# Linear attention: one stage of 16 steps instead of two of 8, first three stacks loaded during the projection, key stacks issued on ScalarE's queue

## The reference

```
def _self_attention(x, w_qkv, w_out, heads):        # 16 heads of 16
    q, k, v = (split(z) for z in jnp.split(x @ w_qkv, 3, axis=-1))
    dots = jnp.einsum('bhie,bhje->bhij', q, k) * d ** (-0.5)
    out = jnp.einsum('bhij,bhje->bhie', dots, v)
    return out.transpose(0, 2, 1, 3).reshape(b, t, d) @ w_out

xh = x.transpose(0, 2, 1, 3).reshape(b * ww, hh, d)   # columns, weights qkv0, out0
oh = _self_attention(xh, w_qkv0, w_out0, HEADS)
xw = x.reshape(b * hh, ww, d)                         # rows, weights qkv1, out1
ow = _self_attention(xw, w_qkv1, w_out1, HEADS)
return oh + ow                                        # x = x + this, on group-normed x
```

## Time and profile before

| | |
|---|---|
| three runs | 2034.88, 2035.12 and 2040.15 us, median 2035.12 |
| span of the profiled execution | 2036.8 us; no other time of it is recorded |
| TensorE busy | 1562.8 us, 77% of the span |
| VectorE, ScalarE, GpSimd busy | 1269.2, 779.2 and 785.0 us |
| mean granted TensorE clock | 0.869 of full speed |
| queue q1 (SP) | 229.35 MB, 36.3% of the 16 transfer engines' span |
| queue q10 (ACT) | 21.31 MB, 3.3% |

### The profile page before, as it was taken

The page is one execution under the profiler, slowest core; times in us unless marked ns, Lnnn a source line. Parts: engine busy times, 40 slices in busy tenths (PEclk is TensorE's granted clock), DMA queues, the critical chain, the costliest instruction groups (busy, mean ns, idle before and its releaser), DMA issues. The chain is left out here.

```text
span 2036.8 us, 38838 instructions
## 1 busy us (share of the span) xinstructions
PE 1562.8 (77%) x13148; PEld 1212.7 (60%) x13148; DVE 1269.2 (62%) x2435; ACT 779.2 (38%) x1652; POOL 785.0 (39%) x956
## 2 busy tenths in 40 slices
PE   5958577649997587791285879947996999999990
PEld 3536464527774344461053546526886999999990
DVE  4846456566664665558224688675664777777776
ACT  2311012305453133451021336622114777777770
POOL 1531102360001440002222250014885887878770
PEclk8968788859998778895598879977997999999995
DMA  2465543354311633219331443114115656666545
GB/s 91 164 166 161 146 115 102 115 168 121 99 48 63 189 84 74 64 19 317 113 88 62 125 141 96 42 39 131 61 65 183 241 206 240 210 229 226 213 156 206
DMA packets 286766, 274.02 MB, mean 135 GB/s; under 512 B 59034, under 2 KB 263677, under 8 KB 280959
## 3 DMA queue, kind: packets, MB, share of 16 engines
q1 hardware_dynamic: 260535, 229.35, 36.3%
q10 hardware_dynamic: 17376, 21.31, 3.3%
q0 software_dynamic: 8688, 21.16, 2.8%
HBM read 194.74 MB, written 79.35 MB: 135 GB/s over the span
## 5 line engine op out<-in xcount | busy, mean ns | idle before, releaser
L787 DVE TENSOR_REDUCE a_maxima<-psum 128x2 f32<-128x512 f32 x384 | 257.5, 687 | 156.4 <-PE psum L578 88.7
L758 ACT ACTIVATE a_probs<-psum 128x512 f32<-128x512 f32 x384 | 224.6, 598 | 262.0 <-PE psum L600 167.8
L89 PE MATMUL psum<-e_x_split,e_up_split 128*128 128x256 f32 x2340 | 311.5, 282 | 7.4 <-DVE e_x_split L1749 7.4
L89 PEld LDWEIGHTS psum<-e_x_split,e_up_split 128*128 128x128 f32 x2340 | 292.5, 189 | 7.8 <-DVE e_x_split L1749 7.8
L1793 POOL TENSOR_TENSOR e_up_split<-e_up_raw,e_up_split 128x512 fp32r<-128x512 f32 x195 | 252.6, 1296 | 90.2 <-ACT e_up_split L1715 88.4
L1685 PE MATMUL psum<-e_down_split,e_hidden_split 128*128 128x256 f32 x1170 | 173.5, 284 | 0.4 <-DVE e_hidden_split L1775 0.4
L578 PE MATMUL psum<-s_k_stack,s_q_stack 96*128 96x256 bf16 x512 | 123.0, 295 | 41.6 <-DMA a_rel_stack<-scr_r 29.7
L1685 PEld LDWEIGHTS psum<-e_down_split,e_hidden_split 128*128 128x128 f32 x1170 | 152.5, 188 | 0.6 <-DVE e_hidden_split L1775 0.6
L1770 DVE TENSOR_TENSOR psum<-psum,e_silu 128x256 f32<-128x256 f32 x195 | 83.8, 430 | 106.8 <-ACT e_silu L1736 106.7
L1754 DVE TENSOR_TENSOR e_down_split<-e_down_raw,e_down_split 128x256 fp32r<-128x256 f32 x195 | 146.3, 750 | 0.0
L1039 DVE TENSOR_TENSOR a_products<-psum,mask 128x512 f32<-128x512 f32 x128 | 82.9, 686 | 78.6 <-PE psum L972 78.4
(11 more groups left out here) (247 smaller groups left out, 3178.1 us busy)
## 6 DMA issues: line engine op xcount, KB each, us to landing
e_up_raw<-in_w_ffn SPq DMA_DIRECT2D x39, 1280.0 KB, 7.4
e_down_raw<-in_w_ffn SPq DMA_DIRECT2D x39, 640.0 KB, 4.2
scr_q<-p_parts SPq DMA_DIRECT2D x40, 384.0 KB, 2.7
scr_k<-p_parts SPq DMA_DIRECT2D x40, 384.0 KB, 2.8
a_q_stack<-scr_q SPq DMA_DIRECT2D x96, 128.0 KB, 2.9
s_q_stack<-scr_q SPq DMA_DIRECT2D x96, 128.0 KB, 2.7
s_k_stack<-scr_k SPq DMA_DIRECT2D x96, 128.0 KB, 2.7
a_k_stack<-scr_k SPq DMA_DIRECT2D x84, 128.0 KB, 3.0
```

Of the source, the lines that this page charges most:

```text
L89: last = eng.matmul(out, lhs(a, k), rhs(b, k), start=i == 0, stop=i == len(terms) - 1)
L758: act.activation(PB[:, u % PR], st_bank(u), ACT.Exp, scale=0.25).then_inc(S["probs"], 1)
L787: dve.tensor_reduce(MX[:, u // 8, :, u % 8], s_bank(u), AX.X, ALU.max).then_inc(S["s_used"], 1)
```

## The change

One phase `a0` with 16 steps n replaces `a0` and `a1`; step n works on image n % 8 of half n // 8. Both output weights are loaded at its start, and the wait for them moves to the first output product. The stacks and their semaphores (one for each side and ring place) live in a `LinearStacks` object that is made before the projection and closed after the attention, in one more clearing block.

During the projection, in steps n = 2 to 6, SP issues one query piece after each spill and ScalarE one key piece after each query or key copy: 18 each, the stacks of images 0 to 2. In the attention SP issues only query stacks, from image 3, each after the scores of the image three before it. ScalarE issues the key stack of image n + 2 in two groups of three, behind its two copies of step n. No stack waits any more for the one before it to land.

```
+                        if linear is not None and 0 <= ahead(n, u) < RING * len(PAIRS):   # SP, behind each spill
+                            image, pair = divmod(ahead(n, u), len(PAIRS))                 # ahead = 4 * (n - 2) + u
+                            if pair == 0:
+                                for of in range(2):
+                                    sp.wait_ge(spilled[of], 16 * (image // 2 + 1))
+                            linear.load_query(sp, image, pair)
...
+                            linear.load_key(act, image, pair)      # the same on ACT, behind each L366 copy, spilled 2 and 3
...
             def _(sp):
-                load_stack(sp, 0, 0)
-                sp.dma_start(WR[:], wo.rearrange("(k p) n -> p k n", p=P)).then_inc(S["w_loaded"], 16)
-                for b in range(1, IMAGES):
-                    if b >= RING:
-                        sp.wait_ge(S["st_done"], (b - RING + 1) * PAIRS_OF)
-                    for j in range(2):
-                        sp.wait_ge(S[("q_stacked", "k_stacked")[j]], per_stack * b)
-                        load_stack(sp, b, j)
+                for j, (_, wo, _) in enumerate(jobs):
+                    sp.dma_start(WR[:, j], wo.rearrange("(k p) n -> p k n", p=P)).then_inc(S["w_loaded"], 16)
+                for n in range(RING, STEPS):
+                    sp.wait_ge(S["st_done"], (n - RING + 1) * PAIRS_OF)
+                    for i in range(len(PAIRS)):
+                        stacks.load_query(sp, n, i)
...
+                    if n == 0:
+                        pe.wait_ge(S["w_loaded"], 16 * len(jobs))      # in project_out
...
-                pe.wait_ge(S["w_loaded"], 16)
-                for b in range(IMAGES):
+                for n in range(STEPS):
...
             def _(act):
-                load_stack(act, 0, 1)
...
                         act.activation(dst, bank, ACT.Copy).then_inc(S["ct_ready"], 1)
+                        ahead = n + RING - 1
+                        if n and ahead < STEPS:
+                            if half == 0:
+                                act.wait_ge(S["st_done"], n * PAIRS_OF)
+                            for i in range(3 * half, 3 * half + 3):
+                                stacks.load_key(act, ahead, i)
...
-        attend_linear(nc, G, "a0", G["v0"], scr["q0"], scr["k0"], A["L0_conv_w_out0"], by_columns=True)
-        attend_linear(nc, G, "a1", G["U"], scr["q1"], scr["k1"], A["L0_conv_w_out1"])
+        attend_linear(nc, G, "a0", [(G["v0"], A["L0_conv_w_out0"], True), (G["U"], A["L0_conv_w_out1"], False)], linear)
+        linear.phase.__exit__(None, None, None)
```

More of the change, by code:

```diff
@@ L297, in feat, with ahead @@
             return (QF, KF)[u // 2][:, u % 2, block * BLOCK:(block + 1) * BLOCK]
+        def ahead(n, u):
+            return 4 * (n - 2) + u
         def v_tiles(n, h):
@@ L366, in _ @@
                             act.activation(feat(u, n), ps[:, u, :], ACT.Copy).then_inc(f_ready, 1)
+                        if linear is not None and 0 <= ahead(n, u) < RING * len(PAIRS):
+                            image, pair = divmod(ahead(n, u), len(PAIRS))
+                            if pair == 0:
+                                for of in range(2, 4):
+                                    act.wait_ge(spilled[of], 16 * (image // 2 + 1))
+                            linear.load_key(act, image, pair)
                     if not bias:
@@ L907, in _, with __init__, load_query, load_key @@
                         copy_v(b, quad)
-def attend_linear(nc, G, name, vt, scr_q, scr_k, wo, by_columns=False):
+class LinearStacks:
+    def __init__(self, nc, name, jobs):
+        self.jobs, self.phase = jobs, Phase(nc, name)
+        self.q = self.phase.sbuf("q_stack", [P, RING, HEADS, SEQ], BF16)
+        self.k = self.phase.sbuf("k_stack", [P, RING, HEADS, SEQ], BF16)
+        self.q_stacked, self.k_stacked = ([self.phase.sem(f"{s}_stacked{r}") for r in range(RING)] for s in "qk")
+    def load_query(self, eng, n, i):
+        self.load(eng, self.q, self.jobs[n // IMAGES][0], PAIRS[i][0], n, i).then_inc(self.q_stacked[n % RING], 16)
+    def load_key(self, eng, n, i):
+        self.load(eng, self.k, self.jobs[n // IMAGES][1], PAIRS[i][1], n, i).then_inc(self.k_stacked[n % RING], 16)
+    def load(self, eng, stack, scr, part, n, i):
+        r = slice(i, i + len(PAIRS) * (DH - 1) + 1, len(PAIRS))
+        src = scr[part, :, bass.ds(n % IMAGES * SEQ, SEQ)].rearrange("(h c) t -> c h t", c=DH)
+        return eng.dma_start(stack[r, n % RING, :, :], src)
+def attend_linear(nc, G, name, jobs, stacks):
     X, ps, masks = G["X"], G["psum"], G["mask"]
-    RING = 3
     PAIRS_OF = HEADS // 2
     HALF = HEADS // 2
+    STEPS = IMAGES * len(jobs)
+    QS, KS = stacks.q, stacks.k
+    q_stacked, k_stacked = stacks.q_stacked, stacks.k_stacked
     with Phase(nc, name) as ph:
-        QS = ph.sbuf("q_stack", [P, RING, HEADS, SEQ], BF16)
-        KS = ph.sbuf("k_stack", [P, RING, HEADS, SEQ], BF16)
         VS = ph.sbuf("v_image", [P, 2, HEADS, 2, DH])
@@ L971, in scores @@
                             tokens = slice(t * P, (t + 1) * P)
[L972 to L973 removed]
+                            last = pe.matmul(st_bank(p)[:, u, t, :], KS[0:STACK, n % RING, 2 * p + u, tokens],
+                                             QS[0:STACK, n % RING, 2 * p + u, tokens], start=True, stop=True)
@@ L974, in scores, with values @@
                     last.then_inc(S["st_done"], 1)
[L976 to L981, removed]
+                def values(n, half):
+                    c = 2 * n + half
+                    pe.wait_ge(S["v_copied"], c + 1)
+                    pe.wait_ge(S["masked"], (c + 1) * PAIRS_OF // 2)
+                    if c >= 2:
+                        pe.wait_ge(S["ct_ready"], c - 1)
@@ L982, in values @@
                     for t in range(2):
                         for side in range(2):
[L984 to L987, removed]
+                            for quarter in range(4):
+                                u = half * HALF + 2 * quarter + side
+                                last = pe.matmul(ps[32 * quarter:32 * quarter + 32, 4 + half, t * P:(t + 1) * P],
+                                                 v_of(n)[:, t, u].rearrange("p s d -> p (s d)"), PB[:, u, t, :],
@@ L1001, in _ @@
-                for b in range(IMAGES):
+                for n in range(STEPS):
                     for p in range(PAIRS_OF):
[L1003 to L1007, removed]
+                        scores(n, p)
+                        if p == 1 and n:
+                            values(n - 1, 1)
+                        if p == 4 and n:
+                            project_out(n - 1)
@@ L1008, in _ @@
                         if p == 5:
-                            values(b, 0)
-                values(IMAGES - 1, 1)
-                project_out(IMAGES - 1)
+                            values(n, 0)
+                values(STEPS - 1, 1)
+                project_out(STEPS - 1)
             @block.scalar
             def _(act):
-                load_stack(act, 0, 1)
-                for b in range(IMAGES):
+                for n in range(STEPS):
                     for half in range(2):
-                        act.wait_ge(S["pv_done"], 2 * b + half + 1)
-                        if b >= 2:
-                            act.wait_ge(S["out_done"], b - 1)
+                        act.wait_ge(S["pv_done"], 2 * n + half + 1)
+                        if n >= 2:
+                            act.wait_ge(S["out_done"], n - 1)
@@ L1049, in _ @@
                 pool.wait_ge(S["setup"], 2)
-                for b in range(IMAGES):
+                for n in range(STEPS):
+                    vt, b = jobs[n // IMAGES][0], n % IMAGES
                     for half in range(2):
-                        if b >= 2:
-                            pool.wait_ge(S["pv_done"], 2 * (b - 2) + half + 1)
+                        if n >= 2:
+                            pool.wait_ge(S["pv_done"], 2 * (n - 2) + half + 1)
                         src = vt[:, 2 * b:2 * b + 2, half * P:(half + 1) * P].rearrange("p t (h s d) -> p t h s d", s=2, d=DH)
@@ L2087, in program @@
         values_tensor("v0")
+        linear = LinearStacks(nc, "s0", [(scr["q0"], scr["k0"]), (scr["q1"], scr["k1"])])
         with attention_inputs() as part:
```

68 lines of the change are left out of this document (32 added, 36 removed).

## The result

The changed kernel took 2018.29 us (median of four runs, 2014.14 to 2024.42) beside 2035.43 for the kernel before on the same chip: ratio 0.9909, 95% interval 0.9884 to 0.9933. It is faster by 0.9% or 17 us, about half of the 36.1 us that the prediction gave, and above the end of its range. The profiled run was the slowest of the four, 2024.42 us.

What follows compares the result with a forecast made beforehand. It took TensorE to bound the projection, and SP's DMA issue pace (8.63 us a step) and two-queue bursts the attention. Savings of 42.1 us, less 1.0 and 5.0, gave -36.1 from 2035.1: 1999.0 us, range 1986 to 2014.

Steps and rivals of the forecast that it cites:

- first start: Attention's start: the first score can go some 0.1 us after the barrier, without the wait for the weight; -11.0 us.
- inner steps and border of the halves: Attention: 12 inner steps become 97.55 us, minus 6.0, and the border between the halves becomes 16.0, minus 21.2.
- projection: Loads among the spills make VectorE wait for spills, so the projection ends later: plus 5 us, between 0 and 10.
- limit (c): Attention step: loop from values product through copy and key issues to the next scores, 3.5 + L, 6.5 or 8.8 us.
- ordinary step P: Time of one attention step for one image: taken as 8.0 us, range 7.4 to 8.8.
- L: Landing time of a key piece in the attention loop: 3.0 us in the middle of all pieces, 5.3 with both queues bursting.
- gain and loss cancel: Rival, chance 0.02: at the longest landing of 7.2 the loop makes P 10.7 us; 2034 us, no change.
- Limit (b): Attention step: transferring an image's twelve 128 KB pieces at 206 GB/s takes 7.6 us.
- limit (a): Attention step without DMA waits: 7.41 us, with TensorE still idle 1.36 us for the mask products.
- Two queues move no more than one: Rival, chance 0.28: attention steps stay at 8.63 us or go to 8.8; 2007 to 2009 us, up to 2017.
- The transfers hide: Rival, chance 0.17: keys land in time, P is 7.4 us and the projection loses 2; 1988 us.
- ScalarE blocks: Rival, chance 0.03: long DMA issues hold up ScalarE's copies in the attention.

Runs made afterwards that it cites:

- e7: The change with SP's query burst held back by six more score products of the next image; 2006.85 us, ratio 0.9840 to the kernel before.
- e2: The change with each group of three key pieces issued one context copy earlier; 1997.11 us, ratio 0.9784 to the kernel before.
- e1: The change without loads during the projection, stacks 0 to 2 issued at the attention's start; 2031.05 us, ratio 0.9962 to the kernel before.
- e3: The change with each projection step's query pieces issued behind its four spills instead of between them; 2012.69 us, ratio 0.9872 to the kernel before.
- e4: The change with key stacks of images 3 to 15 back on SP's queue behind the query stacks; 2003.25 us, ratio 0.9827 to the kernel before.
- e8: The change with the edits of e2 and e3 together; 1988.80 us, ratio 0.9752 to the kernel before.

## Why the prediction was wrong

| term of the sum | predicted | measured |
|---|---|---|
| first start | -11.0 | -10.92 (11.11 to 0.19) |
| first image | -3.9 | -3.87 (11.07 to 7.20) |
| inner steps and border of the halves | -27.2 | -12.65 (140.72 to 128.07) |
| tail | +1.0 | +0.6 (14.2 to 14.80) |
| projection | +5.0 | +8.98 |
| sum, to n2's start | -36.1 | -17.86 |

*The step that failed is limit (c) of the ordinary step P, the term L.* The prediction saw the loop, wrote it as 3.5 + L, and chose P = 8.0, which is L = 4.5, between the middle of all pieces, 3.0, and the burst on two queues, 5.3. The prediction had named its sign, key waits of over 1 us; seven of the nine waits are. Of the 18.2 us that n2's start lacks, 14.5 are in the steps and 4.0 in the projection. The first steps show the loop closing. ScalarE's issues in the kernel after:

```profile
148.15 2.01 ACTq L947 DMA_DIRECT2D s_k_stack<-scr_k  x3
151.57 0.61 ACT L1055 ACTIVATE a_context_t<-psum 128x256 f32<-128x256 f32 x1 [2.81 <-PE psum L1016]
151.57 1.91 ACTq L947 DMA_DIRECT2D s_k_stack<-scr_k  x3
...
162.79 2.18 ACTq L947 DMA_DIRECT2D s_k_stack<-scr_k  x3
```

The values product of 150.43 ends at 151.51, and the second key group of image 3 starts at 151.57. Two issues of 0.64 (a third of 1.91) put its last piece at 152.85. The scores that need it start at 159.84, 7.0 us later, and the next values product follows at 160.78. That is a step of 10.35 us, or 3.4 + 7.0. The value was in the rows: 7.2 is the longest landing of the earlier trace rows, and "gain and loss cancel" was priced with it, at a chance of 0.02. What was missed is which landing a loop picks. The three pieces of that group landed after 5.1, 5.1 and 6.9 us, so their middle is near the 5.3 of the earlier trace rows, but the scores wait for the last. The median over all pieces is made up mostly of pieces that nobody waits for. The pieces that count are those behind the second copy, and they are issued while SP issues six queries for the image just finished. e7 moves the queries, and the longest landing falls to 5.2. After a long wait that burst is over when the next group is issued, at 162.79, and that group lands in time. This fits the alternation of long and short steps; why later steps alternate less I did not follow up. So P came out at 9.22, which in the prediction's 3.5 + L is a mean L of 5.7 where it had 4.5, and 13 x 1.22 = 15.9 us of the miss are here.

*The lost clock is a part of this, as the prediction's last paragraph allowed.* Steps behind a wait run partly at the low level: the 14 steps have a granted clock of 0.87, in e2 of 0.99.

*Limit (b) was too careful.* It took 206 GB/s for a ceiling. In e2 the 12 steps behind the first that still have loads to move ran at 216 GB/s:

```profile
150.28:238.11 87.83, 71.73 (x1248) 59.46 (x1249) 67.90 (x109) 12.12 (x24) 18.25 (x96) 1.00 1.02 216
```

With (c) out of the way P is limit (a): 7.41 predicted, and in e2 7.38 measured in the half of the columns and 7.23 in that of the rows. *The first step* was 8.23 rather than 9.55, so 1.3 us were won there.

*The projection's mechanism was right and its size was off:* +9.0 within bounds of 0 to 10, where I took 5. e1 shows that the loads make all of it, and e3 that their order on SP's queue makes 7.9 of it: a spill that lies behind query loads lands late, after up to 6.2 us, and VectorE needs its buffer. I had shared out the bytes over the transfer engines (a third of 4.5 us) instead of reading the queue as a line. VectorE's timeline in the fourth step, which begins at 71.95 in the earlier trace rows, the rest of it in the kernel before, then the kernel after:

```profile
72.73 1.15 DVE L391 CAST p_parts<-QF 128x512 bf16<-128x512 f32 x1 [0.37 <-DMA scr_q<-p_parts]
...
74.99 0.60 DVE L391 CAST p_parts<-KF 128x512 bf16<-128x512 f32 x1 [0.69 <-DMA scr_k<-p_parts]
...
81.55 0.42 DVE L391 CAST p_parts<-QF 128x512 bf16<-128x512 f32 x1
```

```profile
72.78 0.42 DVE L407 CAST p_parts<-QF 128x512 bf16<-128x512 f32 x1
...
75.30 0.43 DVE L407 CAST p_parts<-QF 128x512 bf16<-128x512 f32 x1 [2.10 <-DMA scr_q<-p_parts]
...
78.18 0.43 DVE L407 CAST p_parts<-KF 128x512 bf16<-128x512 f32 x1 [2.45 <-DMA scr_k<-p_parts]
...
79.97 0.43 DVE L407 CAST p_parts<-KF 128x512 bf16<-128x512 f32 x1 [1.37 <-DMA scr_k<-p_parts]
...
85.48 0.43 DVE L407 CAST p_parts<-QF 128x512 bf16<-128x512 f32 x1
```

The prediction expected a longer wait for the fourth spill alone. Three of four casts now wait, 5.9 us together where it was 1.1, and the step takes 12.70 us where it took 9.60, longer than TensorE's 10.7.

*The rivals.* "Two queues move no more than one" has a number nearer to the time (up to 2017), but e2 refutes its rate, which would have held P at 8.63. Its upper end was reckoned from the loop with an L of 5.9, and that is close to what came: it belongs to the loop and not to the rate. "The transfers hide" is what e2 shows of the steps. "ScalarE blocks", that long issues hold up ScalarE's copies, did not come: its issues in the attention had a median of 0.63 us and a longest of 0.92. The rule of the Trainium skill (DMA: Bandwidth & Descriptors, Issuing engines are not separate DMA queues), that issuing from several engines saves issue time alone, agrees with the runs in what is saved, but not in calling it usually small: here it is the difference between e4's step of 8.20 us and e2's 7.37, once the keys are issued in time.

## What to carry to other kernels

Where a load is issued behind a step's own result and needed in the next step, work out the loop with the landing that those very pieces get, beside the bursts that run at that moment, not with the median of all; where the loop is longer than the step, issue one place earlier before looking for bandwidth. A store whose buffer somebody waits for goes ahead of prefetches on its queue. Read a prefetch that is "hidden" by idle transfer engines again by queue: the idle share says nothing on what stands in line.

## What the runs showed of the hardware

- Loads of 512-byte rows from two queues moved 200 GB/s over 103 us (e2, e8) with the transfer engines 0.93 to 0.96 busy, and 216 over 87.83 us without the first and the last of these steps (e2). With the later keys on one queue (e4) it was 182 GB/s over 14 steps at 0.66, while SP issued almost without a pause (7.8 to 9.1 us for an image):

```profile
139.65:253.23 113.58, 89.92 (x1457) 73.55 (x1457) 79.79 (x127) 14.10 (x28) 20.54 (x108) 0.94 0.66 182
```

- A DMA issue on ScalarE that stands behind a copy in the program starts with the copy and not behind it: copy and issue both begin at 151.57 in the rows above. The 0.49 us of the copy that the prediction put into its loop were not spent.
- The issue of a spill itself grew where loads stood ahead of it on SP: the key spills' median is 0.67 us in the change and 0.36 in the kernel before and in e3.
